# Attention kernel on one core: keys by pieces and weights by chunks in the first batch, attention's first scores pulled into the last projection batch

## The chip, the cores and the metric

The kernel runs on one core of a Trainium2 chip. The metric is the device time of one execution in microseconds (us). Engines are named as the profile names them: PE (matmul) and PEld (its weight loads), DVE (VectorE), ACT (ScalarE), POOL (GpSimd), SP (SyncE, which here only issues DMAs).

## The reference

One transformer block over 8 sequences of 512 tokens, 512 features, 16 heads of 32. All in float32:

```python
z = layernorm(x)
q = split(z @ Wq.T + bq); k = split(ctx @ Wk.T + bk); v = split(ctx @ Wv.T + bv)
scores = einsum("bhqd,bhkd->bhqk", q, k) / sqrt(32)
scores = where(mask == 0, -1e9, scores) + attn_bias
x = x + (softmax(scores) @ v) @ Wo.T + bo
x = x + gelu_ffn(layernorm(x)) + routed_low_rank(layernorm(x))
```

## The kernel before

Three stages follow one another, each a function with a block of its own: `project`, `attend` and `blend`. Between two blocks all five engines meet at a barrier; no engine starts the next function until the last one has left the one before. Inside a block each engine runs its own list of instructions in the written order, and only semaphores (`wait_ge`, `then_inc`) tie the lists together. Nothing is scheduled by a planner.

`project` loops over the 8 batches. A float32 product is made exact enough by splitting both factors into a high part (ACT copies to fp32r) and a low part (DVE subtracts), and by three passes high*high, low*high, high*low. So each of the 12 output tiles of a batch (4 of keys `K_AT`, 4 of values `V_AT`, 4 of queries `Q_AT`) takes 4 chunks x 3 passes = 12 matmuls of 128x512. The 12 tiles go through 4 PSUM banks `ps_j`; a bank is free again once ACT has moved a key tile out (`k_done`) or DVE a value or query tile (`bank_free`). Between keys and values PE transposes the normalised x (16 transposes, L549), between values and queries it does one matmul that spreads the mask factor of each row (`fac_diag`, L559). That factor comes from DVE: mask to `pos` (L430), row minimum (L433), `q_fac` (L437), four diagonals (L440).

In the first batch the weights come in too. The key weights and the first context arrive as four pieces of 128x512 each (L325, L326), are split piece by piece (L513, L514 on ACT, L464, L467 on DVE), and PE waits piece by piece in the first key tile only. The value weights and the query weights come whole, into a buffer that is later used for the mask and into `pos`; ACT copies each in one instruction of 128x2048 (L479) and DVE subtracts in one (L395). SP waits for the low part of the value weights (`w_low`) before it issues the first mask, WoT and all that follows.

WoT and, in every batch, two blocks of W1 and W2 are split as well, the low part on POOL (`wf_l`, L375 and L383, 128x2048).

In the last batch the kernel already prepares `attend`: SP loads q, k, `pos` and bias tiles for the first steps (`load_ahead`, `load_bias`), and POOL makes the first two mask tiles (L356, L360), `pos - bias` for four heads each.

`attend` walks 8 rounds of 16 steps; a step (the code says quad) is 128 queries of one batch and 4 heads. In step j PE makes the scores of its 4 heads (L785), which run side by side in the array, DVE adds the mask tile and takes the row minimum (L873, four), ACT takes the exponential (L932), PE transposes the result in the next step (L796), ACT and DVE copy it out (L913, L880), and PE multiplies with v (L810). All scores use one set of 4 PSUM banks: PE may start the scores of a step only when DVE has done all four minima of the step before (`summed`). POOL makes the mask tile of each step (L750) in a ring of 4 tiles; the tile of step j may be started when step j-4 has been transposed. In odd steps up to 11 DVE does one of the four heads itself.

## Time and profile before

| | |
|---|---|
| time, median of 3 runs | 1814.23 us (1812.32 to 1818.21) |
| profiled execution | 1813.97 us, of which its span 1812.1 us |
| PE busy | 1786.0 us, 99% of the span |
| DVE, ACT, POOL busy | 1039.6, 815.5, 833.0 us |
| `project` | 0 to 291 us of the span |
| `attend` | from 291 us on |
| DMA | 339.97 MB, mean 188 GB/s over the span |

Times in the trace are counted from the start of the span. A timeline row has the start, the duration, the engine, the line, the operation, output and inputs, and in brackets how long the engine stood idle before it and what ended that. A row with a count merges neighbours of one kind. Matmuls are pipelined: a 128x512 matmul is shown as 0.39 us long while the next starts 0.227 us later.

### The profile page before, as it was taken

What the parts mean: (1) busy time and instruction counts of PE and PEld (TensorE: products, weight loads), DVE (VectorE), ACT (ScalarE), POOL (GpSimd) and SP (SyncE); (2) the same over time, 40 slices, a digit from 0 to 9 for tenths busy, and PEclk for the clock granted to TensorE, in tenths of its full rate; (3) what the DMA queues carried; (4) which work ended last, traced back from release to release, by engine and by line L of the source; (5) the groups of instructions that cost most, each with busy time, mean ns of one, the idle gap of its engine ahead of it and who ended that gap; (6) DMA issues with size and microseconds to landing.
All of it is one profiled execution on the core that took longest, in us unless ns stands there. A gap on an engine that the chain in (4) does not pass through costs nothing.

```text
span 1812.1 us, 29631 instructions
## 1 busy us (share of the span) xinstructions
PE 1786.0 (99%) x10784; PEld 1335.4 (74%) x10784; DVE 1039.6 (57%) x2431; ACT 815.5 (45%) x1814; POOL 833.0 (46%) x371
## 2 busy tenths in 40 slices
PE   8999998999999999999999999999999999999999
PEld 6888885555555555555778888888888888888887
DVE  6565556999999999998842334224332242342411
ACT  4222224999999999998232212113131131311300
POOL 1211127999999999997221231222312322223211
PEclk9999998999999999999999999999999999999999
DMA  8998999445436426330543554535546355464453
GB/s 292 339 359 315 324 335 376 144 140 192 136 121 207 140 95 233 105 119 19 200 131 117 199 179 162 203 123 191 180 140 231 123 187 174 138 210 163 150 187 128
DMA packets 198142, 339.97 MB, mean 188 GB/s; under 512 B 10608, under 2 KB 52208, under 8 KB 197488
## 3 DMA queue, kind: packets, MB, share of 16 engines
q1 hardware_dynamic: 194736, 325.50, 53.1%
q0 software_dynamic: 3264, 12.58, 1.9%
q8 instruction: 88, 1.44, 0.3%
q14 instruction: 54, 0.44, 0.1%
HBM read 268.84 MB, written 69.21 MB: 187 GB/s over the span
## 4 chain that ended last, share of the span: by engine, by line
PE 50%; DVE 1%; ACT 0%; issue 0%; POOL 0%; DVEq 0%
PE n_ps_y L1572 19%; PE n_ps_h L1551 19%; PE n_ps_m L1475 9%; PE n_ps_y L1475 3%; PE n_ps_m L1469 1%; DVE k_x L1318 0%; DVE h_bias L1237 0%; DVE k_x L1173 0%; PE n_ps_y L1469 0%; PE n_ps_h L1524 0%; PE n_ps_h L1527 0%; DVE h_k L1246 0%; DVE n_stats L1176 0%; POOL n_g_l L1145 0%; ACT L1431 0%
## 5 line engine op out<-in xcount | busy, mean ns | idle before, releaser
L1145 POOL TENSOR_TENSOR n_g_l<-h_pos,n_g_h 128x512 fp32r<-128x512 f32 x128 | 175.2, 1369 | 602.8 <-DVE n_g_h L1326 602.8
L1551 PE MATMUL n_ps_h<-n_zT_h,n_w 128*128 128x512 f32 x1024 | 336.7, 390 | 1.4 <-ACT h_pos L1431 1.4
L1572 PE MATMUL n_ps_y<-n_w,n_g_h 128*128 128x512 f32 x1024 | 316.6, 390 | 0.3 <-POOL n_g_l L1145 0.3
L1431 ACT ACTIVATE h_pos<-n_ps_h 128x512 f32<-128x512 f32 x128 | 75.8, 599 | 512.4 <-PE n_ps_h L1551 512.3
L1326 DVE CAST n_g_h<-h_pos 128x512 fp32r<-128x512 f32 x128 | 55.3, 434 | 379.5 <-ACT h_pos L1431 379.5
L1551 PEld LDWEIGHTS n_ps_h<-n_zT_h,n_w 128*128 128x128 f32 x1024 | 192.3, 188 | 41.5 <-issue 1.8
L1572 PEld LDWEIGHTS n_ps_y<-n_w,n_g_h 128*128 128x128 f32 x1024 | 191.2, 188 | 39.7 <-POOL n_g_l L1145 0.7
L1572 PE MATMUL n_ps_y<-n_w,n_g_l 128*128 128x512 f32 x512 | 199.3, 389 | 0.0
L1551 PE MATMUL n_ps_h<-n_zT_l,n_w 128*128 128x512 f32 x512 | 199.2, 389 | 0.0
L932 ACT ACTIVATE l_tiles<-l_tiles,a_nmax 128x512 f32<-128x512 f32 x256 | 182.6, 717 | 13.9 <-DVE a_nmax L873 13.9
L932 ACT ACTIVATE a_t_s<-a_t_s,a_nmax 128x512 f32<-128x512 f32 x256 | 182.8, 718 | 0.0
L880 DVE COPY a_pT<-a_ps_t 128x512 f32<-128x512 f32 x256 | 164.6, 684 | 2.1 <-PE a_ps_t L796 2.1
L913 ACT ACTIVATE a_pT<-a_ps_t 128x512 f32<-128x512 f32 x256 | 151.7, 592 | 27.4 <-PE a_ps_t L796 24.7
L873 DVE CUSTOM_DVE_ANT_0 l_tiles<-a_ps_s,l_tiles 128x512 f32<-128x512 f32 x233 | 149.2, 687 | 20.5 <-PE a_ps_s L785 19.6
L796 PEld LDWEIGHTS a_ps_t<-ident,l_tiles 128*128 128x128 f32 x1024 | 111.0, 142 | 64.7 <-issue 47.8
L873 DVE CUSTOM_DVE_ANT_0 a_t_s<-a_ps_s,a_t_s 128x512 f32<-128x512 f32 x232 | 148.6, 688 | 14.6 <-PE a_ps_s L785 10.4
L796 PEld LDWEIGHTS a_ps_t<-ident,a_t_s 128*128 128x128 f32 x1024 | 109.8, 141 | 63.9 <-issue 47.0
L785 PE MATMUL a_ps_s<-h_k,h_q 32*128 32x512 f32 x1024 | 147.9, 647 | 7.0 <-DVE a_nmax L873 3.2
L810 PE MATMUL a_ps_o<-a_pT,a_v 128*32 128x256 f32 x2048 | 149.9, 388 | 0.0
L796 PE MATMUL a_ps_t<-ident,l_tiles 128*128 128x128 f32 x1024 | 141.0, 281 | 0.3 <-ACT a_pT L913 0.3
L796 PE MATMUL a_ps_t<-ident,a_t_s 128*128 128x128 f32 x1024 | 139.4, 279 | 0.3 <-ACT a_pT L913 0.2
L750 POOL TENSOR_TENSOR l_tiles<-a_pos,h_bias 128x2048 f32<-128x2048 f32 x24 | 109.7, 4570 | 11.9 <-PE a_ps_t L796 11.9
(198 smaller groups left out, 3158.2 us busy)
## 6 DMA issues: line engine op xcount, KB each, us to landing
n_w<-wf_d SPq DMA_DIRECT2D x256, 512.0 KB, 4.2
a_pos<-pos_d SPq DMA_DIRECT2D x24, 1024.0 KB, 5.6
l_tiles<-in_x SPq DMA_DIRECT2D x8, 1024.0 KB, 10.1
l_bias<-in_mask SPq DMA_DIRECT2D x8, 1024.0 KB, 14.4
k_d<-p_k_s SPq DMA_DIRECT2D x8, 1024.0 KB, 12.1
pos_d<-p_pos SPq DMA_DIRECT2D x8, 1024.0 KB, 13.4
v_d<-p_v_s SPq DMA_DIRECT2D x32, 256.0 KB, 6.6
wf_d<-p_wf_h SPq DMA_DIRECT2D x16, 512.0 KB, 5.8
```

The costliest lines, as they stand in the source:

```text
L750: pool.tensor_tensor(out=t_s[j % NN][:, first:end, :], in0=pos_rows(b, qt, qt + 1).broadcast_to([P, end - first, S]), in1=bias_rows(first, ...
L785: pe.matmul(ps_s[:, i, :], q[rows, b, qt * P:(qt + 1) * P], k[rows, b, :], start=True, stop=True).then_inc(scored, 1)
L796: last = pe.transpose(ps_t[:, BANK[i], kt * P:(kt + 1) * P], t_s[at[1] % NN][:, i, kt * P:(kt + 1) * P], ident[:, :])
L810: last = pe.matmul(ps_o[rows, :], v[:, b, kt, rows], pT[:, h, i, kt, :], start=kt == 0, stop=kt == NT - 1)
L873: dve.tensor_tensor_reduce(t_s[j % NN][:, i:i + 1, :], ps_s[:, i:i + 1, :], added, 1.0, 3.0e38, ALU.add, ALU.min, nmax[:, j % NN, i:i + 1] ...
L880: dve.tensor_copy(dst, src).then_inc(kept_dve, 1)
L913: act.activation(dst, src, ACT.Copy).then_inc(kept_act, 1)
L932: act.activation(t_s[j % NN][:, i, :], t_s[j % NN][:, i, :], ACT.Exp, scale=-1.0, bias=nmax[:, j % NN, i:i + 1], accum_out=total[:, j // 2 ...
L1145: pool.tensor_tensor(out=g_l[:, f % NG, :], in0=g_f[:, f % NG, :], in1=g_h[:, f % NG, :].bitcast(F32), op=ALU.subtract).then_inc(g_low, 1)
L1475: last = pe.matmul(dst, stationary, moving, start=start and n == 0, stop=stop and n == len(passes) - 1)
L1551: last = pe.matmul(ps_h[:, f % 2, :], stationary, moving, start=i == 0, stop=i == len(passes) - 1)
L1572: last = pe.matmul(ps_y[:, t, :], gs[i], w2[:, f % NW, j, :], start=f == 0 and m == 0, stop=f == NF - 1 and m == 2)
```

## The change

In the first batch:

- `x` is loaded after the second piece instead of after the fourth. DVE does the low parts of pieces 2 and 3 only after the statistics of x (`pieces`).
- `first_keys`: PE runs the 48 key matmuls piece by piece over all four output tiles, high parts first, so that each part is waited for by itself. All four key tiles are complete only at the end.
- PE begins with 8 float32 matmuls of 128x128 whose result nobody reads.
- The value and query weights are split in four chunks of 128x512 on ACT and DVE; PE waits chunk by chunk in the first value tile. SP waits for the fourth chunk (`w_low` counts chunks now).
- DVE moves value tiles 0 and 1 out around the split of the query weights, before the mask work (`values`); tiles 2 and 3 stay behind it. PE's factor matmul (`factors`) comes after the second query tile, only in this batch.

In the last batch:

- PE makes the scores of step 0 after the first query tile and the scores of step 1 after the last (`scores`). DVE takes the minima of step 0 between the first and the second query tile (`first_minima`), ACT its exponentials at the end of the batch. `attend` skips what is done.
- POOL makes the third mask tile too, after the low part of W1 and W2 (`third_mask_tiles`). Its buffer was a tile of `attend` and is now shared with `k_s`, so that it waits for the store of the keys.
- The fourth bias tile is loaded by `project` instead of by `attend`. It goes into the buffer of `pos`, so SP first waits until `pos` has been stored, and it stands ahead of the stores of v.

The number of matmuls, minima, exponentials and DMAs of the two stages is otherwise the same. The core of the diff:

```diff
+        self.tiles = [sb("tiles0"), sb("tiles1"), sb("tiles2")]
+        self.bias = [sb("bias1"), sb("bias2"), sb("bias3")]
+        self.small = sb("small", (P, 8 * HG))
+        self.nmax = self.small[:, 0:4 * HG].rearrange("p (n h) -> p n h", h=HG)
+        self.total = self.small[:, 4 * HG:8 * HG].rearrange("p (a b h) -> p a b h", a=2, b=2)
+        self.ps = stack.enter_context(nc.psum_tensor("l_ps", [P, HG, S], F32))
+        self.scored, self.summed, self.exped = (
+            stack.enter_context(nc.semaphore("l_" + n)) for n in ("scored", "summed", "exped"))
...
-        c_raw, m_raw = late.bias
+        x_raw, xn, k_s = late.tiles
+        c_raw, m_raw, pos = late.bias
...
+                if not more:
+                    sp.wait_ge(pos_out, 16 * (B + 1))
+                    load_bias(3)
...
-            load_x(0)
+                if c == 1:
+                    load_x(0)
...
-            sp.wait_ge(w_low, 1)
+            sp.wait_ge(w_low, NC)
...
+            def third_mask_tiles():
+                pool.wait_ge(ahead.bias_in[2], 16)
+                pool.wait_ge(k_out, 16 * (B + 1))
+                pool.tensor_tensor(out=late.tiles[2][:, :, :], in0=ahead.pos[:, 2:3, :].broadcast_to([P, HG, S]),
+                                   in1=late.bias[1][:, :, :], op=ALU.subtract).then_inc(ahead.nbm_pool, HG)
...
+            def pieces(first, end):
+                for c in range(first, end):
+                    dve.wait_ge(piece_high, 2 * c + 1)
+                    dve.tensor_tensor(out=w_l[1][:, c, :], in0=xn[:, c, :], in1=w_h[1][:, c, :].bitcast(F32),
+                                      op=ALU.subtract).then_inc(piece_low, 1)
+                    dve.wait_ge(piece_high, 2 * c + 2)
+                    dve.tensor_tensor(out=cT_l[:, c, :], in0=c_raw[:, c, :], in1=cT_h[:, c, :].bitcast(F32),
+                                      op=ALU.subtract).then_inc(piece_low, 1)
+
             def weight_low(k):
                 n, raw, _, _ = staging[k]
-                dve.wait_ge(w_high, k + 1)
-                dve.tensor_tensor(out=w_l[n][:, :, :], in0=raw, in1=w_h[n][:, :, :].bitcast(F32),
-                                  op=ALU.subtract).then_inc(w_low, 1)
+                for c in range(NC):
+                    dve.wait_ge(w_high, NC * k + c + 1)
+                    dve.tensor_tensor(out=w_l[n][:, c, :], in0=raw[:, c, :], in1=w_h[n][:, c, :].bitcast(F32),
+                                      op=ALU.subtract).then_inc(w_low, 1)
+
+            def values(b, first, end):
+                for t in range(first, end):
+                    n = V_AT + t
+                    dve.wait_ge(projected, NPJ * b + n + 1)
+                    if t == 0:
+                        dve.wait_ge(v_out, 16 * NC * (b + 1))
+                        if b == 0:
+                            dve.wait_ge(small_in, 48)
+                    dve.tensor_tensor(out=v_s[:, t, :], in0=ps_j[:, n % NPB, :], in1=bv_r[:, :], op=ALU.add) \
+                        .then_inc(bank_free, 1)
...
+            def first_minima():
+                for i in range(HG):
+                    dve.wait_ge(late.scored, i + 1)
+                    dve.wait_ge(ahead.nbm_pool, HG)
+                    gate(dve, passed)
+                    dve.tensor_tensor_reduce(late.tiles[0][:, i:i + 1, :], late.ps[:, i:i + 1, :],
+                                             late.tiles[0][:, i:i + 1, :], 1.0, 3.0e38, ALU.add, ALU.min,
+                                             late.nmax[:, 0, i:i + 1]).then_inc(late.summed, 1)
...
+                if b == 0:
+                    pieces(NC // 2, NC)
...
+                    values(b, 0, 1)
                     weight_low(1)
-                    dve.wait_ge(w_low, 2)
+                    values(b, 1, 2)
+                    dve.wait_ge(w_low, 2 * NC)
...
+                values(b, 0 if b else 2, NT)
...
+                    if not more and c == 0:
+                        first_minima()
...
-                act.activation(w_h[n][:, :, :], raw, ACT.Copy).then_inc(w_high, 1)
+                for c in range(NC):
+                    act.activation(w_h[n][:, c, :], raw[:, c, :], ACT.Copy).then_inc(w_high, 1)
...
+                    for i in range(HG):
+                        act.wait_ge(late.summed, i + 1)
+                        act.activation(late.tiles[0][:, i, :], late.tiles[0][:, i, :], ACT.Exp, scale=-1.0,
+                                       bias=late.nmax[:, 0, i:i + 1], accum_out=late.total[:, 0, 0, i:i + 1]) \
+                            .then_inc(late.exped, 1)
...
+            for _ in range(8):
+                pe.matmul(ps_t[:, 0, 0:P], ones[:, :], ident[:, :], start=True, stop=True)
+
+            def factors(b):
+                pe.wait_ge(diag_done, NT * (b + 1) + 1)
+                pe.wait_ge(xT_low, NC * b + 1)
+                pe.matmul(ps_t[:, 0, :], ones_r[:, :], fac_diag[:, :, :].rearrange("p t n -> p (t n)"),
+                          start=True, stop=True).then_inc(fac_turned, 1)
+
+            def first_keys():
+                for k in range(NC):
+                    for f, (m, n) in enumerate(((0, 0), (1, 0), (0, 1))):
+                        if m + n == 0:
+                            pe.wait_ge(piece_high, 2 * k + 2)
+                        else:
+                            pe.wait_ge(piece_low, 2 * k + (1 if m else 2))
+                        for c in range(NC):
+                            if k == 0 and f == 0:
+                                pe.wait_ge(bank_free, c + 1)
+                            last = pe.matmul(ps_j[:, c, :], (w_h[1], w_l[1])[m][:, k, c * P:(c + 1) * P],
+                                             (cT_h, cT_l)[n][:, k, :], start=k == 0 and f == 0,
+                                             stop=k == NC - 1 and f == len(PASSES) - 1)
+                            if k == NC - 1 and f == len(PASSES) - 1:
+                                last.then_inc(projected, 1)
+
+            def scores(qt):
+                for i in range(HG):
+                    rows = slice(i * DK, (i + 1) * DK)
+                    pe.matmul(late.ps[:, i, :], ahead.q[rows, 0, qt * P:(qt + 1) * P], ahead.k[rows, 0, :],
+                              start=True, stop=True).then_inc(late.scored, 1)
...
-                        if b == 0 and n == K_AT and k % len(PASSES) == 0:
-                            pe.wait_ge(piece_low, 2 * (k // len(PASSES)) + 2)
+                        if b == 0 and n == V_AT and k % len(PASSES) == 0:
+                            pe.wait_ge(w_low, k // len(PASSES) + 1)
...
-                pe.wait_ge(diag_done, NT * (b + 1) + 1)
-                pe.wait_ge(xT_low, NC * b + 1)
-                pe.matmul(ps_t[:, 0, :], ones_r[:, :], fac_diag[:, :, :].rearrange("p t n -> p (t n)"),
-                          start=True, stop=True).then_inc(fac_turned, 1)
-                pe.wait_ge(w_low, 2)
+                if b > 0:
+                    factors(b)
+                pe.wait_ge(w_low, 2 * NC)
                 pe.wait_ge(xT_low, NC * (b + 1))
                 for c in range(NC):
                     product(Q_AT + c, features((w_h[0], w_l[0]), (xT_h, xT_l), c))
+                    if b == 0 and c == 1:
+                        factors(b)
+                    if not more and c == 0:
+                        pe.wait_ge(ahead.qk_in[0], 32)
+                        pe.wait_ge(fac_row_done, B)
+                        scores(0)
+                if not more:
+                    pe.wait_ge(late.summed, HG)
+                    scores(1)
...
-            sp.dma_start(bias_rows(0, HG, 3), bias[0, 0:HG, 3 * P:4 * P, :].rearrange("h p n -> p h n")) \
-                .then_inc(ahead.bias_in[3], 16)
...
-                        if g or j > 1:
+                        if g or j > 2:
...
-                    for i in range(HG):
+                    for i in range(HG if g or j > 1 else 0):
```

In `attend`, DVE and ACT leave out the first step in the same way (`if more and (g or j):`).

DVE in the first batch, from the low part of the value weights to the low part of the next context. Before:

```order
L395 TENSOR_TENSOR p_wv_l<-l_bias,p_wv_h 128x2048 [waits p_w_high]
L422 TENSOR_TENSOR p_xT_l<-p_ps_t,p_xT_h 128x512 [waits p_xT_high] x4
L395 TENSOR_TENSOR p_wq_l<-p_pos,p_wq_h 128x2048 [waits p_w_high]
L430 TENSOR_SCALAR p_pos<-l_bias 128x2048 [waits p_pos_out,p_m_in,p_w_low]
L433 TENSOR_REDUCE p_pos_min<-p_pos 128x4 [waits p_pos_done]
L437 TENSOR_SCALAR p_q_fac<-p_pos_min 128x4 [waits p_min_done]
L440 TENSOR_SCALAR p_fac_diag<-ident,p_q_fac 128x128 [waits p_fac_done]
L440 TENSOR_SCALAR p_fac_diag<-ident,p_q_fac 128x128 x3
L447 TENSOR_TENSOR p_v_s<-p_ps_j,p_bv_r 128x512 [waits p_v_out,p_projected]
L447 TENSOR_TENSOR p_v_s<-p_ps_j,p_bv_r 128x512 [waits p_projected] x3
L400 TENSOR_TENSOR p_cT_l<-l_bias,p_cT_h 128x2048 [waits p_cT_high]
```

Now:

```order
L421 TENSOR_TENSOR p_wv_l<-l_bias,p_wv_h 128x512 [waits p_w_high] x4
L472 TENSOR_TENSOR p_xT_l<-l_ps,p_xT_h 128x512 [waits p_xT_high] x4
L432 TENSOR_TENSOR p_v_s<-p_ps_j,p_bv_r 128x512 [waits p_small_in,p_v_out,p_projected]
L421 TENSOR_TENSOR p_wq_l<-l_bias,p_wq_h 128x512 [waits p_w_high] x4
L432 TENSOR_TENSOR p_v_s<-p_ps_j,p_bv_r 128x512 [waits p_projected]
L482 TENSOR_SCALAR l_bias<-l_bias 128x2048 [waits p_pos_out,p_m_in,p_w_low]
L485 TENSOR_REDUCE p_pos_min<-l_bias 128x4 [waits p_pos_done]
L489 TENSOR_SCALAR p_q_fac<-p_pos_min 128x4 [waits p_min_done]
L492 TENSOR_SCALAR p_fac_diag<-ident,p_q_fac 128x128 [waits p_fac_done]
L492 TENSOR_SCALAR p_fac_diag<-ident,p_q_fac 128x128 x3
L432 TENSOR_TENSOR p_v_s<-p_ps_j,p_bv_r 128x512 [waits p_projected] x2
L437 TENSOR_TENSOR p_cT_l<-l_bias,p_cT_h 128x2048 [waits p_cT_high]
```

Two value tiles have moved ahead of the mask work, one of them ahead of the query weights, and the weights are four instructions each.

SP in the last batch, from the second bias load to the barrier and behind it. Before:

```order
L262 DMA l_bias<-in_bias 128x4x512
L309 DMA v_d<-p_v_s 128x4x128 [waits p_bank_free]
L309 DMA v_d<-p_v_s 128x4x128 x3
...
L319 DMA q_d<-p_q_s 128x512 [waits p_bank_free] x2
L149 UNCONDITIONAL_BRANCH [waits p_v_out,p_k_out,p_pos_out]
L673 UNCONDITIONAL_BRANCH [waits barrier_Pool_Activation_PE_DVE_SP_release]
L695 DMA a_bias<-in_bias 128x4x512
L683 DMA a_v<-v_d 128x4x128
L676 DMA a_pos<-pos_d 128x4x512
```

Now:

```order
L266 DMA l_bias<-in_bias 128x4x512
L266 DMA l_bias<-in_bias 128x4x512 [waits p_pos_out,p_bank_free]
L316 DMA v_d<-p_v_s 128x4x128 x4
...
L326 DMA q_d<-p_q_s 128x512 [waits p_bank_free] x2
L155 UNCONDITIONAL_BRANCH [waits p_v_out,p_k_out,p_pos_out]
L759 UNCONDITIONAL_BRANCH [waits barrier_Pool_Activation_PE_DVE_SP_release]
L769 DMA a_v<-v_d 128x4x128
L762 DMA a_pos<-pos_d 128x4x512
```

The load of the fourth bias tile has moved from behind the barrier to ahead of the v stores, and it waits for `p_pos_out`.

PE from the end of the last query tile into `attend`. Before:

```order
L534 MATMUL p_ps_j<-p_xT_h,p_wq_l 128x512
L149 UNCONDITIONAL_BRANCH
L770 UNCONDITIONAL_BRANCH [waits barrier_Pool_Activation_PE_DVE_SP_release]
L785 MATMUL a_ps_s<-h_k,h_q 128x512 [waits h_qk_in0]
L785 MATMUL a_ps_s<-h_k,h_q 128x512 x3
L785 MATMUL a_ps_s<-h_k,h_q 128x512 [waits a_summed]
L785 MATMUL a_ps_s<-h_k,h_q 128x512 x3
L796 MATMUL a_ps_t<-ident,l_tiles 128x128 [waits a_exped]
```

Now:

```order
L612 MATMUL p_ps_j<-p_xT_h,p_wq_l 128x512
L597 MATMUL l_ps<-h_k,h_q 128x512 [waits l_summed]
L597 MATMUL l_ps<-h_k,h_q 128x512 x3
L155 UNCONDITIONAL_BRANCH
L854 UNCONDITIONAL_BRANCH [waits barrier_Pool_Activation_PE_DVE_SP_release]
L882 MATMUL a_ps_t<-ident,l_tiles 128x128 [waits l_exped,h_qk_in0]
L882 MATMUL a_ps_t<-ident,l_tiles 128x128 x3
L882 MATMUL a_ps_t<-ident,l_tiles 128x128 [waits l_exped]
```

The second scores stand ahead of the barrier; behind it PE starts with transposes of step 0, whose exponentials are done by then.

## Rows read from the trace of the kernel before

**Rows 1.** The profile's page, its first part: busy time and share of PE.

```profile
PE 1786.0 (99%) x10784; PEld 1335.4 (74%) x10784; DVE 1039.6 (57%) x2431; ACT 815.5 (45%) x1814; POOL 833.0 (46%) x371
```

**Rows 2.** Timeline of PE, first batch (start, us, then what).

```profile
7.13 0.63 PE L534 MATMUL p_ps_j<-p_cT_l,p_wk_h 128*128 128x512 f32 x1
...
11.54 0.50 PE L534 MATMUL p_ps_j<-p_cT_h,p_wk_h 128*128 128x512 f32 x1
...
21.65 1.97 PE L549 MATMUL p_ps_t<-ident,l_tiles 128*128 128x128 f32 x16 [0.97 <-DVE l_tiles L416]
23.85 0.50 PE L534 MATMUL p_ps_j<-p_wv_h,p_cT_h 128*128 128x512 f32 x1 [0.23 <-DVE p_wv_l L395]
...
46.03 0.39 PE L534 MATMUL p_ps_j<-p_cT_h,p_wk_h 128*128 128x512 f32 x1
```

**Rows 3.** Timeline of PE around the barrier into attention.

```profile
288.75 0.39 PE L534 MATMUL p_ps_j<-p_xT_h,p_wq_l 128*128 128x512 f32 x1
291.27 2.09 PE L785 MATMUL a_ps_s<-h_k,h_q 32*128 32x512 f32 x8 [2.14 <-PEq L149]
296.12 2.09 PE L785 MATMUL a_ps_s<-h_k,h_q 32*128 32x512 f32 x8 [2.76 <-DVE a_nmax L873]
...
301.71 1.14 PE L785 MATMUL a_ps_s<-h_k,h_q 32*128 32x512 f32 x8
...
314.51 1.14 PE L785 MATMUL a_ps_s<-h_k,h_q 32*128 32x512 f32 x8
```

**Rows 4.** Busy time, 292 to 296 us; after POOL: clock, DMA share, GB/s.

```profile
292.00:296.00 4.00, 1.36 (x8) 0.00 (x0) 2.46 (x8) 1.73 (x5) 4.00 (x4) 0.50 1.02 340
```

**Rows 5.** Timeline of ACT, first batch.

```profile
18.03 1.92 ACT L479 ACTIVATE p_wv_h<-l_bias 128x2048 fp32r<-128x2048 f32 x1 [7.35 <-DMA l_bias<-in_WvT]
19.85 2.40 ACT L492 ACTIVATE p_k_s<-p_ps_j,p_bk_c 128x512 f32<-128x512 f32 x4
```

**Rows 6.** Timeline of SP, first batch.

```profile
23.82 0.37 SPq L240 DMA_DIRECT2D l_bias<-in_mask  x1
```

**Rows 7.** Timeline of all engines, 29 to 40 us, PE and SP left out.

```profile
29.22 1.23 DVE L430 TENSOR_SCALAR p_pos<-l_bias 128x2048 f32<-128x2048 int32 x1 [0.68 <-DMA l_bias<-in_mask]
...
33.01 0.87 DVE L440 TENSOR_SCALAR p_fac_diag<-ident,p_q_fac 128x128 fp32r<-128x128 f32 x4
33.27 1.92 ACT L500 ACTIVATE p_wf_h<-p_wf 128x2048 fp32r<-128x2048 f32 x1 [7.06 <-DMA p_wf<-in_WoT]
33.80 2.48 DVE L447 TENSOR_TENSOR p_v_s<-p_ps_j,p_bv_r 128x512 f32<-128x512 f32 x4
35.27 4.63 POOL L375 TENSOR_TENSOR p_wf_l<-p_wf,p_wf_h 128x2048 fp32r<-128x2048 f32 x1 [15.63 <-ACT p_wf_h L500]
...
38.01 4.04 DVE L400 TENSOR_TENSOR p_cT_l<-l_bias,p_cT_h 128x2048 fp32r<-128x2048 f32 x1 [1.73 <-ACT p_cT_h L483]
```

**Rows 8.** Timeline of all engines, 271 to 273 us, PE left out.

```profile
271.70 4.62 POOL L360 TENSOR_TENSOR l_tiles<-h_pos,l_bias 128x2048 f32<-128x2048 f32 x1 [5.83 <-DMA l_bias<-in_bias]
272.28 4.06 DVE L437 TENSOR_SCALAR p_q_fac<-p_pos_min 128x4 f32<-128x4 f32 x1
```

**Rows 9.** Timeline of DVE, the first minimum of attention.

```profile
293.54 0.69 DVE L873 CUSTOM_DVE_ANT_0 l_tiles<-a_ps_s,l_tiles 128x512 f32<-128x512 f32 x1 [3.61 <-PE a_ps_s L785]
```

**Rows 10.** Timeline of SP, last batch.

```profile
279.68 2.87 SPq L309 DMA_DIRECT2D v_d<-p_v_s  x4
...
288.11 2.46 SPq L319 DMA_DIRECT2D q_d<-p_q_s  x2
```

**Rows 11.** DMA issues of 270 to 280 us (KB each, median us to landing).

```profile
pos_d<-p_pos SPq DMA_DIRECT2D x1, 1024.0 KB, 11.0
l_bias<-in_bias SPq DMA_DIRECT2D x1, 1024.0 KB, 13.2
```

**Rows 12.** DMA issues of 292.2 to 292.4 us, columns as in rows 11.

```profile
a_pos<-pos_d SPq DMA_DIRECT2D x1, 1024.0 KB, 8.9
```

**Rows 13.** Groups of POOL (busy us, mean ns | idle before, releaser).

```profile
L750 POOL TENSOR_TENSOR l_tiles<-a_pos,h_bias 128x2048 f32<-128x2048 f32 x24 | 109.7, 4570 | 11.9 <-PE a_ps_t L796 11.9
```

63 lines of the change are left out of this document (26 added, 37 removed).

## The prediction

> **What bounds the kernel now.** I read the page first: PE is busy 99% of the span [rows 1]. So a change elsewhere counts only where PE stands idle or runs slowly, and I looked for these places in PE's timeline. The change touches two: the first batch and the barrier between projection and attention. Two clocks matter: at the full one (2.4 GHz) a 128x512 matmul starts every 0.227 us, as the 97 matmuls from the first value tile to the second batch show, (46.03 - 23.85) / 97 = 0.229 with two small gaps [rows 2]; at the half one (1.2 GHz) the matmul is 0.63 us long instead of 0.39, and the rate is about half.
>
> In the first batch PE waits for pieces, then 0.97 us for the normalised x and, after the transposes, until 23.85 for the whole low part of the value weights; the full clock comes at 11.54 [rows 2]. At the barrier PE ends the projection at 289.0, starts attention at 291.27, makes four heads' scores in 2.09 us, waits 2.76 us for the four minima and makes the next in 2.09. The same scores take 1.14 us at 301.71, when the clock is back [rows 3]; in between the granted clock is 0.50 of full speed [rows 4].
>
> **First batch, keys and x.** Pieces 0 and 1 arrive as before. High times high runs before the low parts, so PE starts about 0.8 us sooner. With x (1 MB) now ahead of pieces 2 and 3, these come some 2.8 us later (1 MB at about 0.37 MB/us, an estimate from the weights' landing), and PE, which takes them in order, ends the keys near 18.9 instead of 20.7; x is normalised by 17.5 to 18.2. The transposes, 1.97 us, end near 20.9. The 8 dummy matmuls stand before the first piece arrives and cost nothing; if they bring the full clock sooner the keys end sooner, but the next wait hides it.
>
> **That wait is ACT.** The value weights land at the same time, because the same bytes stand before them: ACT starts at 18.03 [rows 5]. Four chunks of 128x512 on ACT take between 1.92 (the whole copy) and 2.40 (its four key tiles) [rows 5]; I take 2.2, since a copy is nearer to the first. Only at 20.2 can ACT move the first key tile out (0.6), whose bank the first value tile needs. So values start at 20.95 instead of 23.85: **2.9 us** sooner. Chunks on DVE follow ACT's by 0.7 and are ready at 21.0.
>
> **What takes part of it back.** SP's mask load and WoT wait for that low part: 23.82 before [rows 6], about 21.15 now, 2.65 us earlier. WoT's chain has nothing else in it: ACT's high part starts when WoT has landed (33.27), POOL's low part at 35.27 [rows 7]; both move to about 30.6 and 32.6, and POOL holds until 37.25. DVE's mask work does not move with them. It had to wait 0.68 us for the mask at 29.22 [rows 7]; now the mask is early, but two value tiles (0.62 each [rows 7]) stand ahead of it, and it starts near 29.0. Scaled, minimum and `q_fac` take it to 32.6, so the four diagonals (0.87) now meet POOL's instruction, where before they ended 1.4 us ahead of it [rows 7]. What such a meeting costs two rows show: `q_fac` in the last batch lasted 4.06 us and ended with POOL's mask tile, and the context's low part 4.04 [rows 7, 8]. So I let the diagonals wait until 37.25. They end at 38.1, value tile 2 is out at 38.8, and its bank is what the third query tile needs. PE, at the end of its second query tile at 20.95 + 72 x 0.227 = 37.3, waits for the factor and then for the bank: 1.6 us in all, of which 0.2 was PE's factor matmul anyway. Query tiles 2 and 3, 24 x 0.227 = 5.4, end at 44.3 instead of 46.03: the first batch brings **1.7 us**. The bounds are 2.9 (no meeting) and 1.0 (diagonals and both value tiles late by another 0.7).
>
> The Trainium skill, "SBUF — State Buffer", section "SBUF: two separate sides", says that DVE and GpSimd share one pair of ports as an exclusive lock, held for the whole instruction, and that the loser blocks fully. By a shared bandwidth instead, the diagonals would only be stretched, and the first batch would bring 2.9. The traced 4.06 us is the lock's number, so the sum follows it.
>
> **Batches 1 to 6** are unchanged and PE fills them; the gain passes through. In the last batch DMA, minima and mask tiles are in the same order up to the query tiles.
>
> **The barrier.** The scores of step 0 (1.14 at the full clock [rows 3]) go into PE's stream; q, k and the factor row are there. DVE takes its four minima (2.5 in all, from the first one's start to the next scores, 296.12 - 293.54 [rows 3, 9]) while PE makes the second query tile (2.72), so the next bank is not late; ACT is idle then. The scores of step 1 follow the last query tile. So PE's projection ends 1.14 later for its last query tile and 2.28 later in all. SP carries the cost: it issues almost without a pause from 279.68 until 290.57 [rows 10], and now first waits for the store of `pos`, landed at 269.95 + 11.0 = 280.95, and issues 1 MB of bias ahead of v [rows 11]. The bias ahead of it lands at 270.37 + 13.2 = 283.6, so the queue stays full and SP is paced by DMA. The barrier opens 1.14 later if PE's query tile is what SP waits for, and 2.8 later if SP is held back by the whole extra MB. I take 1.7, nearer to the first, since part of that MB fills slack: **barrier at 293.0** on the old scale instead of 291.27.
>
> **From the barrier to the scores of step 5**, which stand at 314.51, from where PE is packed again [rows 3]. Now: minima of step 1 2.5 (DVE starts at once; it waited 3.61 for scores before [rows 9]), scores 1.14 + 0.2, minima 2.5, scores 1.34, DVE's copies of step 1 hold it 0.3, minima of step 3 with one head's extra add 3.1, scores 1.34, minima 2.5: 14.9, and 15.5 with the transposes and v products that PE has to fit in. That gives 308.5. Second limit, the mask tile of step 4: its `pos` lands at 292.3 + 8.9 = 301.2 [rows 12], POOL takes 4.6, the minima 2.5, PE at 308.4; DMA was full before (share 1.02 [rows 4]), so the moved bias does not bring `pos` sooner. Both agree; I take 308.7, a gain of **5.8 us**. It is made of the idle 2.14 + 2.76 us, the slow 3 us or so, less 1.7.
>
> **Sum:** 1.7 + 5.8 = 7.5 us off the profiled execution's 1813.97: 1806.5. The median is 0.26 above that execution, so 1806.7. About 0.3% (5.4 us) is what a measurement of this kernel can tell from no change.
>
> **Rivals.**
> 1. *No meeting on the ports.* The diagonals slip ahead of POOL because WoT lands a us later than I reckon, or DVE is a us faster. First batch 2.9, total 8.7, 1805.5. Against it: two independent chains must shift by 1.1 us. Chance 0.16.
> 2. *The clock still falls at the barrier.* PE stood idle for 2.14 us before it fell; now it idles about 1.6 us. If the clock is half for the same 10 us, scores take 2.09 and the first transposes limit PE; I get 310.6 for step 5, 1.9 less gain, total 5.6, 1808.6. For it: the gap is not much shorter. Chance 0.26. The Trainium skill, "TensorE: Matmul & The Clock Gate", Part 1, says that the moment of a change is not tied to the kernel's own start, so that it may differ between runs; no row here shows that.
> 3. *SP's queue eats the start.* The whole MB delays the barrier (2.8) and, through a fuller queue, `pos` of step 4 as well. Another 2.5 to 4 lost, total 4.3, 1809.9, within 0.3%. For it: SP is busy all that time [rows 10]. Chance 0.11.
> 4. *POOL becomes attention's pace: slower.* Before, POOL was ahead of the minima; now the minima of step 4 wait for their tile, and the lead is zero. If POOL doesn't get ahead again, each of 124 further steps waits a little. From 0.06 us a step it eats the 7.5 us, from 0.10 it makes the kernel slower by 5, 1819. Against it: POOL itself idled 11.9 us, for PE, over 24 of its tiles [rows 13], and a full tile of 4.57 alternates with shorter ones over most of a round, against PE's 4.3 us a step ((314.51 - 301.71) / 3 [rows 3]). Chance 0.05.
>
> **Numbers.** The forecast has 0.42. Faster by over 0.3% (below 1808.8): 0.42 + 0.16 and 0.10 of rival 2, 0.68. Within: 0.16 of rival 2 and rival 3, 0.27. Slower: 0.05. The range goes from 1803.0 (rival 1 with runs 2 us under their median, as before) to 1811.0 (rival 3 with a us above).
>
> **What would show it.** First value matmul near 21 and a DVE diagonal or `q_fac` row of about 4 us beside POOL's `wf_l` in the first batch, with PE idle ahead of the third query tile; second batch at 44.3. On the other side no scores row of 2.09 us, PE's idle before the barrier below 2 us, 1.00 in every stretch, and scores of step 5 some 7.5 us sooner than 314.51. Wrong if the diagonals run in 0.87 right away, if the clock reads 0.50 behind the barrier, or if PE waits for mask tiles later in the round.

## The result, and the profile after

The changed kernel takes 1806.88 us, the median of 6 runs (1806.43 to 1807.19), where the kernel before took 1813.97 beside it (6 runs, 1812.32 to 1818.21). The ratio is 0.9965, 95% interval 0.9955 to 0.9975: faster by 0.25 to 0.45%. A control run of it later gave 1806.96 beside 1812.16, ratio 0.9967 (0.9955 to 0.9980). The profiled execution of it took 1806.92, its span is 1805.1; so 7.0 us of span are to be found between the two traces. The kernel before had a high first group: over all 65 of its executions here its median is 1812.76, and over the 11 of the changed kernel 1806.92, which makes the gain 5.8 us.

PE's timeline of the first batch (start, us, then what) answers to [rows 2]:

```profile
1.53 3.79 PE L570 MATMUL l_ps<-ident,ones 128*128 128x128 f32 x16 [1.53 <-POOL ident L355]
...
13.07 1.21 PE L588 MATMUL p_ps_j<-p_cT_h,p_wk_h 128*128 128x512 f32 x4 [1.26 <-ACT p_cT_h L562]
...
19.04 1.91 PE L630 MATMUL l_ps<-ident,l_tiles 128*128 128x128 f32 x16
21.06 0.50 PE L612 MATMUL p_ps_j<-p_wv_h,p_cT_h 128*128 128x512 f32 x1
...
37.55 0.39 PE L575 MATMUL l_ps<-p_fac_diag,p_ones_r 128*128 128x512 f32 x1
37.81 0.50 PE L612 MATMUL p_ps_j<-p_xT_h,p_wq_h 128*128 128x512 f32 x1
...
43.38 0.39 PE L612 MATMUL p_ps_j<-p_cT_h,p_wk_h 128*128 128x512 f32 x1
```

The weight load (PEld) of that first value matmul:

```profile
21.06 0.18 PEld L612 LDWEIGHTS p_ps_j<-p_wv_h,p_cT_h 128*128 128x128 f32 x1 [0.35 <-ACT l_tiles L534]
```

Keys now go piece by piece, four tiles of a pass in one group, and the one long wait, 1.26, is for the third piece. There is no wait ahead of the transposes (0.97 before), and the first value matmul stands at 21.06 instead of 23.85; its weights wait 0.35 for ACT to move the first key tile out. The second batch's keys start at 43.38 instead of 46.03: 2.65 us.

Timeline of all engines, 29 to 39 us, PE and SP left out, answers to [rows 7]:

```profile
29.26 1.22 DVE L482 TENSOR_SCALAR l_bias<-l_bias 128x2048 f32<-128x2048 int32 x1
...
29.59 1.92 ACT L542 ACTIVATE p_wf_h<-p_wf 128x2048 fp32r<-128x2048 f32 x1 [2.83 <-DMA p_wf<-in_WoT]
...
31.59 4.63 POOL L389 TENSOR_TENSOR p_wf_l<-p_wf,p_wf_h 128x2048 fp32r<-128x2048 f32 x1 [16.38 <-ACT p_wf_h L542]
...
32.83 3.42 DVE L489 TENSOR_SCALAR p_q_fac<-p_pos_min 128x4 f32<-128x4 f32 x1
...
36.28 0.88 DVE L492 TENSOR_SCALAR p_fac_diag<-ident,p_q_fac 128x128 fp32r<-128x128 f32 x4
...
37.07 1.28 DVE L432 TENSOR_TENSOR p_v_s<-p_ps_j,p_bv_r 128x512 f32<-128x512 f32 x2
```

`q_fac`, 0.17 us of work, takes 3.42 and ends with POOL's `wf_l` at 36.22. The diagonals follow, and PE's factor matmul stands at 37.55, just where its second query tile ends. So the meeting (a DVE instruction held up while POOL's long one runs) happened and was nearly hidden: from the first value matmul to the second batch's keys it is 22.32 us, 0.2 more than in the kernels without a meeting. In the last batch it was not; DVE, POOL and PE there, which answers to [rows 8]:

```profile
269.64 0.17 DVE L489 TENSOR_SCALAR p_q_fac<-p_pos_min 128x4 f32<-128x4 f32 x1
269.85 5.22 DVE L492 TENSOR_SCALAR p_fac_diag<-ident,p_q_fac 128x128 fp32r<-128x128 f32 x4
```

```profile
270.16 4.63 POOL L368 TENSOR_TENSOR l_tiles<-h_pos,l_bias 128x2048 f32<-128x2048 f32 x1 [6.93 <-DMA l_bias<-in_bias]
```

```profile
275.81 0.47 PE L612 MATMUL p_ps_j<-p_xT_h,p_wq_h 128*128 128x512 f32 x1 [0.19 <-DVE p_v_s L432]
```

Before, `q_fac` was caught and POOL's tile ended in time; now the diagonals are caught, four of them lasting 5.22, and PE starts its first query tile at 275.81 instead of 278.00. Of the 2.65 us 2.19 are left. The value tiles behind the diagonals come late with them, and PE waits 0.19 for a bank.

PE around the barrier, which answers to [rows 3]:

```profile
278.72 1.14 PE L597 MATMUL l_ps<-h_k,h_q 32*128 32x512 f32 x8
...
288.18 1.14 PE L597 MATMUL l_ps<-h_k,h_q 32*128 32x512 f32 x8
291.19 1.07 PE L882 MATMUL a_ps_t<-ident,l_tiles 128*128 128x128 f32 x8 [1.87 <-PEq L155]
...
294.24 2.06 PE L871 MATMUL l_ps<-h_k,h_q 32*128 32x512 f32 x8
...
299.09 1.14 PE L871 MATMUL l_ps<-h_k,h_q 32*128 32x512 f32 x8 [0.43 <-DVE l_small L959]
...
307.93 1.14 PE L871 MATMUL l_ps<-h_k,h_q 32*128 32x512 f32 x8
```

The scores of steps 0 and 1 stand ahead of the barrier, at 1.14 us each. Behind it PE turns step 0 at once instead of waiting 2.76 us for minima. The barrier itself is no sooner (291.19; 291.27 before). The scores of step 5 come at 307.93 instead of 314.51. The clock still falls, as the windows show, the first of which answers to [rows 4] (after POOL: granted clock, DMA share, GB/s):

```profile
291.00:295.00 4.00, 3.56 (x20) 2.78 (x24) 3.79 (x10) 3.15 (x9) 3.78 (x3) 0.71 1.06 397
295.00:300.00 5.00, 4.32 (x32) 2.03 (x24) 3.54 (x11) 3.82 (x11) 0.49 (x1) 0.89 1.00 311
```

POOL and SP, which answer to [rows 10, 12, 13] (a tile in attention; then the queue in the last batch):

```profile
299.51 4.57 POOL L834 TENSOR_TENSOR l_tiles<-a_pos,h_bias 128x2048 f32<-128x2048 f32 x1 [4.60 <-DMA a_pos<-pos_d]
```

```profile
278.34 0.37 SPq L266 DMA_DIRECT2D l_bias<-in_bias  x1
278.75 2.79 SPq L316 DMA_DIRECT2D v_d<-p_v_s  x4
...
288.17 2.16 SPq L326 DMA_DIRECT2D q_d<-p_q_s  x2
```

```profile
L834 POOL TENSOR_TENSOR l_tiles<-a_pos,h_bias 128x2048 f32<-128x2048 f32 x24 | 109.9, 4579 | 12.7 <-PE a_ps_t L882 8.1 <-DMA a_pos<-pos_d 4.6
```

The mask tile of step 4 waits 4.60 us for its `pos` and ends at 304.1. POOL idles 8.1 us for PE over the 24 tiles of that group (11.9 before), so it did not become attention's pace: from the scores of step 5 to the first output projection PE takes 857.75 - 307.93 = 549.82, before 864.00 - 314.51 = 549.49.

**The 7.0 us:** first batch +2.65, lost on the way to the last query tiles -0.46, from there to step 5 +4.39, attention -0.33 (that distance is 549.5 to 550.0 in all traces here, in no order that I could explain), and +0.75 behind attention, where the trace of before has a stretch of half clock at 864 us and this one has none.

### The profile page after: what moved, and what is told of

Its sections match the earlier page's. It is cut to its first block, busy times and chain, and to the rows that moved or that the text cites. A ratio compares the mean times of both kernels' runs of the same rounds, so it can differ in the third digit from the quotient of the medians.

```text
span 1805.1 us, 29668 instructions
## 1 busy us (share of the span) xinstructions
PE 1785.3 (99%) x10800; PEld 1336.1 (74%) x10800; DVE 1041.4 (58%) x2437; ACT 813.9 (45%) x1820; POOL 832.8 (46%) x368
## 4 chain that ended last, share of the span: by engine, by line
PE 51%; DVE 1%; ACT 0%; issue 0%; POOL 0%; DVEq 0%
PE n_ps_y L1658 19%; PE n_ps_h L1637 19%; PE n_ps_m L1561 9%; PE n_ps_y L1561 3%; PE n_ps_m L1555 1%; DVE k_x L1404 0%; DVE h_bias L1323 0%; PE n_ps_y L1555 0%; PE n_ps_h L1610 0%; PE n_ps_h L1613 0%; DVE h_k L1332 0%; POOL n_g_l L1231 0%; ACT L1517 0%; ACT L1500 0%; ACT L1497 0%
## 5 line engine op out<-in xcount | busy, mean ns | idle before, releaser
L1018 ACT ACTIVATE l_tiles<-l_tiles,l_small 128x512 f32<-128x512 f32 x380 | 270.2, 715 | 0.0
L959 DVE CUSTOM_DVE_ANT_0 l_tiles<-l_ps,l_tiles 128x512 f32<-128x512 f32 x357 | 227.4, 687 | 28.2 <-PE l_ps L871 24.1
L882 PEld LDWEIGHTS a_ps_t<-ident,l_tiles 128*128 128x128 f32 x1536 | 165.1, 141 | 92.9 <-issue 74.6
L882 PE MATMUL a_ps_t<-ident,l_tiles 128*128 128x128 f32 x1536 | 209.7, 280 | 2.4 <-PEq L155 1.9
L834 POOL TENSOR_TENSOR l_tiles<-a_pos,l_bias 128x2048 f32<-128x2048 f32 (+1 forms) x48 | 201.6, 4214 | 5.8 <-PE a_ps_t L882 5.7
L871 PE MATMUL l_ps<-h_k,h_q 32*128 32x512 f32 x1008 | 144.7, 643 | 2.2 <-DVE l_small L959 0.4
L1658 PEld LDWEIGHTS n_ps_y<-n_w,n_g_l 128*128 128x128 f32 x512 | 96.1, 188 | 20.0
L1637 PEld LDWEIGHTS n_ps_h<-n_zT_l,n_w 128*128 128x128 f32 x512 | 96.2, 188 | 19.5
L397 POOL TENSOR_TENSOR p_wf_l<-p_wf,p_wf_h 128x2048 fp32r<-128x2048 f32 x8 | 37.0, 4623 | 139.9 <-ACT p_wf_h L551 139.9
```

Of the source, the lines that this page charges most:

```text
L834: pool.tensor_tensor(out=t_s[j % NN][:, first:end, :], in0=pos_rows(b, qt, qt + 1).broadcast_to([P, end - first, S]), in1=bias_rows(first, ...
L871: pe.matmul(ps_s[:, i, :], q[rows, b, qt * P:(qt + 1) * P], k[rows, b, :], start=True, stop=True).then_inc(scored, 1)
L882: last = pe.transpose(ps_t[:, BANK[i], kt * P:(kt + 1) * P], t_s[at[1] % NN][:, i, kt * P:(kt + 1) * P], ident[:, :])
L959: dve.tensor_tensor_reduce(t_s[j % NN][:, i:i + 1, :], ps_s[:, i:i + 1, :], added, 1.0, 3.0e38, ALU.add, ALU.min, nmax[:, j % NN, i:i + 1] ...
L1018: act.activation(t_s[j % NN][:, i, :], t_s[j % NN][:, i, :], ACT.Exp, scale=-1.0, bias=nmax[:, j % NN, i:i + 1], accum_out=total[:, j // 2 ...
L1637: last = pe.matmul(ps_h[:, f % 2, :], stationary, moving, start=i == 0, stop=i == len(passes) - 1)
```

## The experiments

All twelve kernels are measured by the same marks of PE's timeline, each the first matmul of a kind: V the first value tile of the first batch, K2 the second batch's keys, Q8 the last batch's first query tile, then the barrier (PE's first row behind it) and the scores of step 5. The times are medians of 5 to 12 executions; the ratios below the first are against 15 to 25 executions of the kernel before, which had medians of 1812.2 to 1813.0. "Half" is how long the granted clock stood at half within 50 us of the barrier.

| kernel | V | V to K2 | K2 to Q8 | Q8 to barrier | Q8 to step 5 | half, us | time | ratio (95%) |
|---|---|---|---|---|---|---|---|---|
| before | 23.85 | 22.18 | 231.97 | 13.27 | 36.51 | 10.2 | 1813.97 | |
| after | 21.06 | 22.32 | 232.43 | 15.38 | 32.12 | 3.4 | 1806.88 | 0.9965 (0.9955, 0.9975) |
| after_again | 20.40 | 22.54 | 232.51 | 15.65 | 31.11 | 0 | 1806.96 | 0.9967 (0.9955, 0.9980) |
| first_only | 20.90 | 23.34 | 232.44 | 13.27 | 36.67 | 10.2 | 1810.84 | 0.9988 (0.9979, 0.9997) |
| handover_only | 23.04 | 22.12 | 231.92 | 16.51 | 32.81 | 3.4 | 1816.46 | 1.0010 (0.9998, 1.0022) |
| handover_rerun | 21.75 | 22.12 | 231.95 | 15.99 | 33.62 | 6.8 | 1810.93 | 0.9998 (0.9984, 1.0011) |
| handover_true | 22.85 | 22.12 | 231.95 | 15.96 | 32.27 | 3.4 | 1809.28 | 0.9989 (0.9979, 0.9999) |
| no_dummy | 21.11 | 23.17 | 232.13 | 16.00 | 32.50 | 3.4 | 1807.81 | 0.9972 (0.9961, 0.9983) |
| whole_w | 21.60 | 22.13 | 232.97 | 15.43 | 30.90 | 0 | 1807.89 | 0.9972 (0.9961, 0.9983) |
| diag_first | 19.97 | 22.12 | 231.77 | 16.30 | 33.71 | 6.8 | 1806.60 | 0.9967 (0.9954, 0.9979) |
| late_bias3 | 20.45 | 22.39 | 232.51 | 14.76 | 31.10 | 0 | 1806.31 | 0.9966 (0.9953, 0.9978) |
| no_sc1 | 19.98 | 22.77 | 232.43 | 15.71 | 33.12 | 3.4 | 1807.97 | 0.9971 (0.9961, 0.9981) |
| best | 20.59 | 22.12 | 232.59 | 14.65 | 32.40 | 0 | 1805.70 | 0.9962 (0.9949, 0.9974) |
| best_warm | 20.20 | 22.12 | 232.15 | 15.35 | 32.38 | 0 | 1806.60 | 0.9964 (0.9952, 0.9977) |

**The first batch alone (first_only).** Early scores, minima, exps and the third mask tile go, the last bias load goes back into attention:

```diff
-                    if not more and c == 0:
-                        first_minima()
...
-                if not more:
-                    third_mask_tiles()
...
-                        if g or j > 2:
+                        if g or j > 1:
```

> The changed kernel with the first batch's parts alone: no early scores, minima or exps, no third mask tile ahead, the last bias rows loaded in attention again. Theory A (what the changed kernel's trace shows: second batch's keys at 43.38 instead of 46.03, first query tile of the last batch at 275.81 instead of 278.00): the gain is 2.2 to 2.65 us, so 1811.3 to 1811.8; keys of the second batch at 43.4, the first half-clock stretch behind the barrier about 10 us long as before. Theory B (the forecast's term): 1.7 us, 1812.3, with keys of the second batch at 44.3.

1810.84 beside 1812.76: 1.9 us by the medians, near B's 1.7, though the time is below both theories' figures, which count from 1813.97. The trace has the second batch's keys at 44.24, as B says, and the last query tiles at 276.68, 1.3 sooner than before. The first batch is, instruction for instruction, that of the changed kernel; what differs is when WoT landed. DVE, POOL and PE here (ACT starts on WoT at 30.68, in the changed kernel at 29.59):

```profile
32.68 4.66 POOL L386 TENSOR_TENSOR p_wf_l<-p_wf,p_wf_h 128x2048 fp32r<-128x2048 f32 x1 [17.62 <-ACT p_wf_h L535]
32.68 0.17 DVE L484 TENSOR_SCALAR p_q_fac<-p_pos_min 128x4 f32<-128x4 f32 x1
...
32.88 5.12 DVE L487 TENSOR_SCALAR p_fac_diag<-ident,p_q_fac 128x128 fp32r<-128x128 f32 x4
...
38.06 0.50 PE L562 MATMUL l_ps<-p_fac_diag,p_ones_r 128*128 128x512 f32 x1 [0.55 <-DVE p_fac_diag L487]
```

`q_fac` slips through and the diagonals are caught until 37.34; PE's factor matmul waits 0.55 and the third query tile for its bank. V to K2 is 23.34 instead of 22.32. So the forecast's 1.7 us and the 2.65 of the changed kernel's trace are two outcomes of one and the same first batch.

**The last batch alone (handover_only, handover_rerun, handover_true).** Keys tile by tile, x behind the pieces, weights whole, factor matmul ahead of the query tiles, no dummy matmuls; the first two lack before's wait of DVE for the small loads, the third has it:

```diff
-            for _ in range(8):
-                pe.matmul(ps_t[:, 0, 0:P], ones[:, :], ident[:, :], start=True, stop=True)
...
-                for c in range(NC):
-                    act.activation(w_h[n][:, c, :], raw[:, c, :], ACT.Copy).then_inc(w_high, 1)
+                act.activation(w_h[n][:, :, :], raw, ACT.Copy).then_inc(w_high, NC)
...
-            pieces(0, NC // 2)
+            pieces(0, NC)
...
+            dve.wait_ge(small_in, 48)
             walk(dve, body)
```

> The changed kernel with the last batch's parts alone; the first batch is as before (no dummy matmuls, keys tile by tile, x behind the pieces, weights whole, factor matmul ahead of the query tiles, values together). Theory A (the two traces: 4.39 us between the last batch's first query tile and the scores of step 5): the gain is 4.2 to 4.8 us, so 1809.2 to 1809.8. Theory B (the forecast's term): 5.8 us, 1808.2. Theory C (the two parts hinder each other, because the last batch comes sooner against its DMA): the gains of this kernel and of the first batch alone add up to more than the 7.1 us of the whole change, by 0.5 or more.

> The last batch's parts alone, and this time the first batch wholly as before: DVE waits again for the small loads ahead of the statistics of x (the earlier kernel of this kind lacked that wait and started its values at 23.04 instead of 23.85, with whole weights). Theory A: values start at 23.85 and the second batch's keys at 46.0; the fast executions lie 4.2 to 4.8 us below the kernel before. The earlier kernel had executions near 1808.5 and near 1817, 8 us apart; if that comes from the new handover, this one has both levels too and the profile of a late one shows where the 8 us lie; if it came from the first batch's other phase, it has one level.

> The same kernel as handover_only once more, for a trace of one of its executions near 1817 us (8 of 12 were there, 4 near 1809). Theory A (a longer or another stretch of half clock): the clock's mean differs by 0.001 to 0.002 and the late trace shows 7 to 14 us more of half clock. Theory B (attention runs in another phase, in which POOL's mask tiles or ACT's exps come late in each step): the distance from the scores of step 5 to the first output projection is 555 or more instead of 549.5 to 550, at full clock. Theory C (the DMA-heavy end): the distance from there to the end is 955 instead of 947.4 to 949.2.

In the traces the part does what it should: Q8 to step 5 is 32.3 to 33.6 instead of 36.5. In handover_true 9 of 11 executions lie at 1807.96 to 1809.60, 2.6 to 4.2 below the 1812.16 of before, and two at 1815.7. That is short of the 4.2 to 4.8 that both texts expected, although the trace has 4.24 from Q8 to step 5 (36.51 - 32.27). Its median is 2.9 below; with the 1.9 of the first batch alone that makes 4.8 of the control's 5.2. By the medians the parts add up, and nothing speaks for theory C of the first text; the intervals of the two parts (0.5 to 3.8 and 0.2 to 3.8 us) are too wide to exclude its 0.5. The executions at 1815.7 to 1818.3 (8 of 12, 2 of 8 and 2 of 11) had none in the 63 executions whose first batch is the new one (the changed kernel's own among them); before itself has two of 65, 1818.21 and 1820.05. No trace caught one: the three profiled executions have spans of 1809.1, 1807.9 and 1806.7. The recorded mean clocks fit theory A in sign: 0.996 to 0.998 in the late executions of handover_only and its rerun, 0.998 to 0.999 in the others. But 0.002 of 1810 is 3.6 us, and some 7 are to be found, and in handover_true the late ones have 0.998 like most others, so a lower clock is at most a part of it. Theories B and C of the last text stay open, and so does what the new first batch has to do with it. These late executions are also why the first two kernels' medians and ratios say little.

handover_true also says how much luck a start holds: with before's own first batch its values start at 22.85, not at the expected 23.85. The small loads landed sooner, and PE's transposes wait for nothing (0.97 before). DVE's first wait for them, in before's trace and in this one:

```profile
15.25 2.47 DVE L407 BATCH_NORM_STATS2 p_stats<-l_tiles 128x6 f32<-128x512 f32 x4 [3.63 <-DMA p_bv_r<-in_bv]
```

```profile
13.57 2.47 DVE L451 BATCH_NORM_STATS2 l_small<-l_tiles 128x6 f32<-128x512 f32 x4 [2.07 <-DMA p_bv_r<-in_bv]
```

**No dummy matmuls (no_dummy).** The first two lines of the diff above alone.

> The changed kernel without its 8 dummy matmuls. Theory A (hidden: PE has 1.26 us of idle time ahead of the third piece and ACT's key tile sets the start of the values): the granted clock rises near 11 us instead of 6.3, pieces 0 and 1 run at half of it, the keys end up to 0.5 us later, the values start 0 to 0.4 us later, the time is 1806.9 to 1807.3. Theory B (the early clock carries a good part of the first batch's gain): values start over 1 us later, time 1808 or more.

```profile
7.60 1.91 PE L586 MATMUL p_ps_j<-p_cT_h,p_wk_l 128*128 128x512 f32 x4
...
10.55 1.09 PE L586 MATMUL p_ps_j<-p_cT_h,p_wk_h 128*128 128x512 f32 x4
...
19.44 1.91 PE L628 MATMUL l_ps<-ident,l_tiles 128*128 128x128 f32 x16
```

The first passes run at half rate (1.91 for four, against 1.08) until about 9.7 us, the wait of 1.26 ahead of the third piece vanishes, and the keys end 0.4 later than in the changed kernel (19.44 against 19.04); V is 21.11. Against that trace theory A holds for V; the time, 1807.81, is 0.5 above its range. But the transposes start at 18.20 to 19.04 in the nine traces with dummy matmuls and keys by pieces, so 19.44 is the latest of ten, and V is 0.71 later than in the control. The ratio, 0.9972, cannot be told from the control's 0.9967, and its trace has 0.63 more between V and K2, by the meeting on the ports. So these runs leave the worth of the matmuls anywhere from 0 to 0.9 us.

**Weights whole (whole_w).**

```diff
-                for c in range(NC):
-                    act.activation(w_h[n][:, c, :], raw[:, c, :], ACT.Copy).then_inc(w_high, 1)
+                act.activation(w_h[n][:, :, :], raw, ACT.Copy).then_inc(w_high, NC)
```

> The changed kernel with the value and query weights split whole again (one high part, one low part each) and all else as changed. Theory A (the forecast's: chunks alone carry the first batch's gain, keys by pieces carry none of it): the values start at 23.5 to 24.1 instead of 21.06, the second batch's keys at 45.8 to 46.4, time 1809.4 to 1809.9. Theory B (keys by pieces and x ahead carry part of it): values start below 23 and the time is 1808.5 or less.

```profile
18.20 1.91 PE L628 MATMUL l_ps<-ident,l_tiles 128*128 128x128 f32 x16
21.60 0.47 PE L610 MATMUL p_ps_j<-p_wv_h,p_cT_h 128*128 128x512 f32 x1 [1.49 <-DVE p_wv_l L420]
```

Values start at 21.60 with a wait of 1.49 for the low part, not at 23.5 to 24.1 with one of 2.9. Theory A falls, B holds. The 1.5 us are what the chunks are worth to V: in the changed kernel and eight others with both parts that wait is gone and V is 19.97 to 21.11. The rest of V's gain is that PE reaches the transposes sooner, at 18.20 to 19.44 in the traces with keys by pieces and x ahead, at 20.09 to 21.65 in the four without. Since DVE no longer normalises x so late, it is also free sooner for the low part. WoT's load waits for the same whole low part, so ACT starts on WoT at 30.62 instead of 29.14 in the control, while `q_fac` starts at 31.63 instead of 32.17. So the diagonals go ahead of POOL (V to K2 is 22.13), and at the second batch's keys whole_w is 0.8 behind the control (43.73 and 42.94), where V was 1.2 behind.

**The control, and diagonals first (after_again, diag_first).** The first is the changed kernel once more, the second has one more wait of POOL:

```diff
                     pool.wait_ge(wo_high, 1)
+                    pool.wait_ge(diag_done, NT + 1)
```

> The changed kernel itself once more, as a control beside the kernels of this call. If the first batch's meeting of DVE and POOL depends on when WoT lands (29.6 us in the changed kernel's trace, 30.6 us in three others), the second batch's keys start either at 43.4 or near 44.25, nothing in between, and the times spread over 1 to 2 us; the ratio to the kernel before stays between 0.996 and 0.9975. If they always start at 43.4, the 0.86 us belong to the other kernels' edits.

> The changed kernel with one more wait: in the first batch POOL starts the low part of WoT only after DVE's four diagonals. Theory A (the meeting costs PE up to 0.9 us where WoT lands late enough that q_fac or the diagonals run into POOL's instruction just before PE needs the factor): q_fac takes 0.17 and the diagonals 0.88, the query tiles run without a pause, the second batch's keys start at 43.2 to 43.5 whenever WoT lands, and the time is 0.3 to 0.9 us below the changed kernel's of this call. Theory B (the meeting is hidden behind the query tiles anyway): same time as the changed kernel's within 0.3. Theory C (POOL's instruction now delays WoT's store and the feed-forward load behind it and something waits for these): later by 0.5 or more.

The control's keys of the second batch start at 42.94, because V is 0.66 sooner than in the first trace; that text had missed how much V itself varies. Its ratio and its spread (1.5 us) are as expected. DVE and POOL of diag_first:

```profile
31.62 0.17 DVE L490 TENSOR_SCALAR p_q_fac<-p_pos_min 128x4 f32<-128x4 f32 x1
...
31.83 0.88 DVE L493 TENSOR_SCALAR p_fac_diag<-ident,p_q_fac 128x128 fp32r<-128x128 f32 x4
...
32.62 1.28 DVE L433 TENSOR_TENSOR p_v_s<-p_ps_j,p_bv_r 128x512 f32<-128x512 f32 x2
...
32.85 4.63 POOL L390 TENSOR_TENSOR p_wf_l<-p_wf,p_wf_h 128x2048 fp32r<-128x2048 f32 x1 [18.41 <-DVE p_fac_diag L493]
...
33.82 5.81 DVE L438 TENSOR_TENSOR p_cT_l<-l_bias,p_cT_h 128x2048 fp32r<-128x2048 f32 x1
```

This shows the mechanism: 0.17 and 0.88, then POOL, and V to K2 is 22.12, as in every kernel in which nothing meets (22.12 to 22.18; 97 matmuls at 0.228). The kernels in which they meet have 22.32, 22.39, 22.54, 22.77, 23.17 and 23.34. So the meeting costs 0.2 to 1.2 us, and what sets it is how late POOL's instruction ends behind the first value matmul: 15.16 us in the changed kernel (0.20 lost), 15.22 in late_bias3 (0.27), 15.36 in the control (0.42), 15.60 in no_sc1 (0.65), 16.02 in no_dummy (1.05), 16.44 in first_only (1.22). K2 to Q8 is 231.77: in the last batch the diagonals (268.55, 0.87) end here as POOL's tile starts. The time is 1806.60, 0.36 below the control; A's range begins there, but the intervals cannot tell it from B. The barrier opens 16.30 behind Q8 instead of 15.65, and the clock stood at half for 6.8 us. A gain ahead of the barrier is partly waited away at it.

**Without the third mask tile (late_bias3)**, the last bias rows loaded in attention:

```diff
                 if not more:
-                    sp.wait_ge(pos_out, 16 * (B + 1))
-                    load_bias(3)
...
-                if not more:
-                    third_mask_tiles()
```

> The changed kernel without its third mask tile: POOL makes tile 2 after the barrier, and the last bias rows are loaded in attention again, so that 1 MB less stands in SP's queue in the last batch. The early scores, minima and exps stay. Theory A (that 1 MB delays the barrier by 0.9 us of the 2.1 measured, and the tile itself gives back 3 to 4 us that the minima of step 2 would wait for): barrier at 290.3 instead of 291.2, tile 2 heads at 1.15 us each pace the minima of step 2, the scores of step 5 at 308 to 309 instead of 307.9, time within 1 us of the changed kernel's. Theory B (the third tile carries much of the 4.4 us): scores of step 5 at 310 or later, time 2 us or more above the changed kernel's.

```profile
286.79 2.46 SPq L323 DMA_DIRECT2D q_d<-p_q_s  x2
...
290.06 4.99 POOL L831 TENSOR_TENSOR l_tiles<-h_pos,l_bias 128x512 f32<-128x512 f32 x4 [7.79 <-PEq L853]
295.39 3.77 POOL L831 TENSOR_TENSOR a_t_s<-h_pos,l_bias 128x512 f32<-128x512 f32 x3 [0.35 <-DMA l_bias<-in_bias]
299.11 4.58 POOL L831 TENSOR_TENSOR l_tiles<-a_pos,h_bias 128x2048 f32<-128x2048 f32 x1
```

The same two stores of SP in the control:

```profile
287.87 2.37 SPq L326 DMA_DIRECT2D q_d<-p_q_s  x2
```

PE at the scores of step 5 in late_bias3:

```profile
306.45 1.14 PE L868 MATMUL l_ps<-h_k,h_q 32*128 32x512 f32 x8 [0.81 <-DVE l_small L956]
```

The barrier opens 0.9 sooner (14.76 against 15.65), and POOL, with one tile more to do behind it, ends the tile of step 4 at 303.7 instead of 303.4, for which PE waits 0.81: step 5 stands at 31.10 behind Q8, as in the control (31.11). So in this pair of traces, both at full clock, the third mask tile and the megabyte moved for it cancel. Theory A holds on the barrier and the time; its 308 to 309 for step 5 came at 306.45, in a trace without half clock.

What opens the barrier shows in SP's rows. In eleven of the twelve traces with early scores PE's first row stands 0.85 to 0.89 behind the end of SP's last store of q. Without the moved megabyte this store follows PE's last query tile directly: its last matmul starts at 287.42, DVE moves it out until 288.60, the store ends at 289.25, the barrier opens at 290.11. With it SP is behind: DVE is done at 288.70 in the control, the store ends at 290.24.

**Without the second scores (no_sc1).**

```diff
-                if not more:
-                    pe.wait_ge(late.summed, HG)
-                    scores(1)
```

> The changed kernel without the early scores of step 1: they come after the barrier, as the first thing. The early scores, minima and exps of step 0 and the third mask tile stay. Theory A (the second scores carry their own 1.14 us, and the minima of step 1 that DVE can start at the barrier carry some of their 2.5): barrier 14.2 to 14.8 behind the last batch's first query tile instead of 15.4 to 15.7, scores of step 5 32.5 to 34 behind it instead of 31.1 to 32.1, time 1 to 2.5 above the changed kernel's. Theory B (SP's queue sets the barrier whatever PE does): barrier at 15.4 or later and the time 2.5 to 3.6 above.

```profile
290.89 1.22 PE L867 MATMUL l_ps<-h_k,h_q 32*128 32x512 f32 x8 [3.27 <-PEq L155]
```

PE waits 3.27 us at the barrier, which opens 15.71 behind Q8 although PE has 1.14 less to do ahead of it: theory B on the barrier, SP's queue sets it as long as the moved megabyte is in it. The price is A's: 33.12 against 32.12 at the same 3.4 us of half clock, 1.0 us. The time, 1807.97 with a ratio of 0.9971 against the control's 0.9967, is on the same side and within the intervals.

**All that pays (best, best_warm).** The diffs of late_bias3 and diag_first, and one wait in the last batch; best_warm has five matmuls more:

```diff
                 pool.wait_ge(x_turned, NC * B)
+                pool.wait_ge(diag_done, NT * B + 1)
...
                     scores(1)
+                    pe.wait_ge(bank_free, NPB + NVQ * b + NT + 1)
+                    for _ in range(5):
+                        pe.matmul(ps_j[:, Q_AT % NPB, 0:P], ones[:, :], ident[:, :], start=True, stop=True)
```

> The changed kernel without its third mask tile (bias rows 3 loaded in attention again), and with two waits that keep POOL's long instruction behind DVE's diagonals: WoT's low part in the first batch, the second mask tile in the last one. Theory A (each of the three does what the traces of its parts show): 22.1 to 22.2 us from the first value matmul to the second batch's keys instead of 22.3 to 23.3; 231.8 to 232.0 from there to the last batch's first query tile instead of 232.4 to 232.5 (DVE's diagonals took 5.22 there beside POOL); barrier 14.8 behind that tile instead of 15.4 to 15.7. Together 0.7 to 1.5 below the changed kernel, 1805.4 to 1806.3. Theory B (what is gained ahead of the barrier is waited for at it, since SP's queue sets it: with the earlier start of the kernel with the first wait alone it opened 16.3 behind the tile instead of 15.6): nothing beyond the 0.65 us that the kernel without the third tile had, 1806.3 to 1807.

> The kernel called best, with five matmuls of 128x128 on PE behind the scores of step 1, in the place of PE's idle time at the barrier. Theory A (PE's idle time there, 1.9 to 3.0 us in the traces, is what lets the clock fall in most executions, at a price of 1.0 us for 3.4 us of half clock): no half clock between 285 and 310, the first transposes of attention take 1.07 to 1.14 for 8, and the time is 0.3 to 1.0 below best. Theory B (the clock falls, or not, whatever PE does in those 2 us): half clock in this trace or the same time as best. Theory C (the matmuls make PE the last at the barrier): it opens up to 0.5 later.

The time of best is 1805.70 (1804.65 to 1807.84), ratio 0.9962 (0.9949 to 0.9974). The median is in A's range, but the interval holds the changed kernel's ratio, and the profiled execution took 1807.11, so it is not shown to be better. In that trace no meeting is left in either batch, and the barrier opens 14.65 behind Q8, as theory A has it, as early as PE's last query tile allows (287.27, and 2.68 us from there, as in late_bias3). But PE waits elsewhere, 0.54 us in the third batch and 2.14 in attention:

```profile
78.08 0.47 PE L609 MATMUL p_ps_j<-p_cT_h,p_wk_h 128*128 128x512 f32 x1 [0.54 <-DVE p_q_s L501]
```

```profile
307.70 1.14 PE L870 MATMUL l_ps<-h_k,h_q 32*128 32x512 f32 x8 [2.14 <-DVE l_small L958]
```

```profile
a_pos<-pos_d SPq DMA_DIRECT2D x1, 1024.0 KB, 9.5
```

```profile
300.40 4.54 POOL L833 TENSOR_TENSOR l_tiles<-a_pos,h_bias 128x2048 f32<-128x2048 f32 x1 [0.89 <-PE a_ps_t L881]
```

The tile of step 4 starts at 300.40, and the scores of step 5 wait 2.14. The row names PE's transposes, but this tile needs only those of step 0, which end at 292.4. The other thing it needs is its `pos`: the load (the DMA row above: KB, then us from issue to landing) is issued at 290.80 and lands 9.5 us later, at 300.3. In late_bias3 and the control the same load took 7.9 and 7.3 us. So it is the forecast's second limit, the landing of `pos`, that holds step 5 here, and its landing time differs by up to 2.2 us from trace to trace.

PE of best_warm around the barrier:

```profile
287.82 1.38 PE L651 MATMUL p_ps_j<-ident,ones 128*128 128x128 f32 x10
289.82 1.06 PE L884 MATMUL a_ps_t<-ident,l_tiles 128*128 128x128 f32 x8 [0.62 <-PEq L155]
```

With the five matmuls the clock did not fall at the barrier (PE's idle time there is 0.62), but it had not fallen in best, late_bias3 and after_again either, with 1.22 to 2.12 us of idle time, so theories A and B on the clock are not decided by that pair. The price is decided: SP's last store ends at 288.25, PE's five matmuls at 289.20, and the barrier opens 1.57 behind the store instead of 0.86. PE is now the last at the barrier and opens it 0.7 later, as theory C says and more than its 0.5. The median, 1806.60, is 0.9 above best, within the intervals.

## Why the prediction was right, and where not

It gave 1806.7 and the kernel takes 1806.88, the range held it, and the sign was right. The sum of 7.5 stands against 7.0 us of span. Much of that closeness is luck. Its two terms were off in opposite directions, 1.7 against 2.2 us up to the last batch's query tiles and 5.8 against 4.4 from there to step 5. The trace of before holds about 1 us of luck: its small loads landed 1.7 later than in handover_true, and its values started 1.0 later. And the forecast counts from 1814: against the 1812.76 of all 65 executions the gain is 5.8 us, the control's against its own kernel before 5.2, so 7.5 was about 2 too many. Of its own signs of being wrong one came, half clock behind the barrier. The lower end of its range is not its own working either: 1805.5 less 2 is 1803.5, not 1803.0.

- **PE as the bound, the two places, batches 1 to 6:** right. K2 to Q8 is 231.8 to 232.6 in all kernels but whole_w (232.97). Only whole_w and best have a wait of PE between the second and the last batch, 0.24 and 0.54 us, both for DVE's query rows at the third batch's keys.
- **Values at 20.95, keys' end 18.9:** 21.06 and 19.04. The step "that wait is ACT" holds in this trace: the first value matmul's weights wait for ACT's first key tile, and V stands 2.82 behind ACT's first chunk of the value weights (18.24). The same 2.82 is in the control, first_only and no_sc1. In the other five traces with keys by pieces and chunks ACT is early enough, and V stands 1.66 to 1.67 behind the first transpose. The 2.9 us have two sources that the forecast did not tell apart: with whole weights the wait for their low part is 1.49 (whole_w), and the pieces' order and x give the rest.
- **The meeting on the ports, bank of the third query tile late by 1.6, gain 1.7:** the mechanism is shown by diag_first. Keys of the second batch at 44.3 were right for first_only (44.24) and no_dummy (44.28); in the profiled execution WoT had landed a us sooner than I reckoned, POOL ended at 36.2 instead of 37.25, and 2.65 came. That is near rival 1's 2.9, by way of an earlier WoT, where I had asked for a later one.
- **"The gain passes through" to the last batch:** wrong by 0.46. The bias rows for POOL's tile, and so the tile, came sooner by only 1.54 (270.16 for 271.70), DVE's mask work by 2.64, and the tile fell on the diagonals (5.22). diag_first has none of this loss.
- **Barrier 1.7 later:** 2.1, and 2.4 in the control. Both ingredients are as named: 1.49 without the moved megabyte (late_bias3), where PE's last query tile sets it through SP's last store, and 0.9 for the megabyte, with which SP's queue sets it (no_sc1).
- **Step 5 at a gain of 5.8:** 4.39 in the trace. At full clock it is 36.51 - 31.11 = 5.40 in the control. So 1.0 is the clock, and the remaining 0.4 fits the barrier, later by 0.4 to 0.7 than priced.
- **Rival 2, the clock still falls, chance 0.26:** it came in the profiled execution, in a smaller size: 3.4 us instead of 10. Of twelve traces with the early scores seven have such a stretch (3.4 or 6.8 us), five none. I had asked whether it falls; it is a matter of the execution.
- **Rival 3** had the right place for the cost at the barrier and too large an amount. **Rival 4** did not come: 549.8 against 549.5 us over attention.

## What to carry to other kernels

Where a change moves one of two independent chains that share a port, its gain is a lottery of who comes first; a wait that fixes the order takes the lottery out, which in the first batch here was worth 0.2 to 1.2 us of PE's timeline, though the times of these runs are too coarse to show it. Ahead of a barrier ask which queue reaches it last, and what that queue itself waits for: what other engines gain there is waited away, work moved ahead of it (the third mask tile) is paid with the transfer that it pulls along, and filler work can make its own engine the last (best_warm). A single trace of the kernel before can hold a us of luck in its first loads, as much as the terms that are weighed here, so read a first batch from two.

## What was not expected of the hardware

- **The clock differs between executions of one program.** The changed kernel's stretch of half clock behind the barrier was 3.4 us long in one trace and absent in its control; handover_only had 3.4, its rerun 6.8. From the barrier to the scores of step 5 these pairs take 16.74 against 15.46 and 17.63 against 16.30: 1.3 us for 3.4 us of half clock. (From Q8 it is 1.0 and 0.8, since the barrier itself opened at other distances.) With before's handover it was 10.2 us in both traces. A second stretch, behind attention, costs less: from the first output projection to the end it is 947.4 in four traces without it and 947.7 to 948.1 in eight with it (handover_only with it and its rerun without it, 949.2 and 948.4, stand apart). The Trainium skill, "TensorE: Matmul & The Clock Gate", Part 1, says that the moment of a change is not tied to the kernel's start; by these pairs the traces agree. With a clock that moves by itself, one trace of each kernel can't price a term of 1 us here.
- **Full clock on paper.** In no_dummy the profile grants 1.00 from 6 to 10 us, while groups of four 128x512 matmuls take 1.91 instead of 1.08. In the first us of a kernel the durations tell the clock, not its row.
- **Not every DVE instruction is held by POOL.** Beside POOL's 4.63 at 32.85 in diag_first, two value tiles (sum of PSUM and an SBUF row) took 1.28, as ever, while the low part of the context, with two SBUF inputs, took 5.81 instead of 2.28. The Trainium skill, "SBUF — State Buffer", section "Who interferes with whom", holds that a DVE instruction with at most one SBUF input, outside the two-port modes, does not contend; these rows agree. The diagonals and `q_fac`, which have one SBUF tensor, were held (5.12 and 3.42), so by that rule they ran in one of those modes, which no row here shows.
